# A two-layer transformer megakernel: layer 1's feed-forward one chunk later, and its convolution, residual addition and modulation in another order

## The reference, cut to what matters

```python
x = x + attn(cond(x, c))            # cond: modulated norm (scale, shift from c), 16-head attention of
                                    # width 16, o + o @ W_out; attn: layer norm, 16 rotary query heads
                                    # of width 128, one key/value head, causal softmax, @ Wo
y = causal_depthwise_conv(x, c)     # 32 taps per channel: 32 lags over 32 tokens
x = x + (relu(y @ w_fc) ** 2) @ w_proj     # 256 -> 1024 -> 256, weights block-quantised
```

## Time and profile before

| | us |
|---|---|
| median of 3 runs (lowest, highest) | 1431.28 (1430.86, 1431.62) |
| the profiled execution | 1429.93 |
| its span, first to last instruction | 1428.1 |
| busy in it: PE, DVE, ACT, POOL | 1306.4, 1125.2, 781.8, 137.8 |
| mean granted clock of PE | 0.974 |

### The profile page before, as it was taken

The page is one execution under the profiler, slowest core; times in us unless marked ns, Lnnn a source line. Parts: engine busy times, 40 slices in busy tenths (PEclk is TensorE's granted clock), DMA queues, the critical chain, the costliest instruction groups (busy, mean ns, idle before and its releaser), DMA issues.

```text
span 1428.1 us, 25862 instructions
## 1 busy us (share of the span) xinstructions
PE 1306.4 (91%) x9475; PEld 929.7 (65%) x9490; DVE 1125.2 (79%) x2892; ACT 781.8 (55%) x1486; POOL 137.8 (10%) x153
## 2 busy tenths in 40 slices
PE   5999999979799999999999858899999999999997
PEld 2444444658687877778777535566677767676766
DVE  4899999778968686786869798587869696969785
ACT  3999888854455565656555644534353434444213
POOL 0000000101010101011011110001010202020100
PEclk9999999989999999999999979898999999999999
DMA  9333333520111010202022300000000000000000
GB/s 380 105 71 74 71 89 87 148 95 31 38 38 46 31 46 31 73 4 75 21 104 85 129 24 1 28 11 8 9 19 3 22 0 22 7 8 8 8 8 15
DMA packets 26518, 73.97 MB, mean 52 GB/s; under 512 B 3992, under 2 KB 5156, under 8 KB 25136
## 3 DMA queue, kind: packets, MB, share of 16 engines
q1 hardware_dynamic: 25840, 71.62, 16.0%
q10 hardware_dynamic: 576, 0.98, 0.2%
HBM read 49.52 MB, written 23.07 MB: 51 GB/s over the span
## 4 chain that ended last, share of the span: by engine, by line
PE 51%; DVE 36%; ACT 6%; issue 6%; DMA 1%; DVEq 0%; SPq 0%; ACTq 0%; POOL 0%
PE psum L613 12%; PE psum L722 6%; DVE work L1811 5%; PE psum L934 5%; PE psum L661 4%; DVE ffn_mem L1928 4%; DVE h_all L1811 3%; DVE work L1942 3%; PE psum L963 3%; PE psum L973 3%; PE psum L880 2%; PE psum L626 2%; PE psum L671 2%; PE psum L647 1%; PE psum L567 1%
## 5 line engine op out<-in xcount | busy, mean ns | idle before, releaser
L613 PE MATMUL psum<-h_all,w_big 128*128 128x256 f32 x1024 | 244.1, 387 | 9.7 <-ACT work L1259 9.7
L613 PEld LDWEIGHTS psum<-h_all,w_big 128*128 128x128 f32 x1024 | 190.3, 192 | 49.4 <-issue 14.3
L1811 DVE SCALAR_TENSOR_TENSOR work<-work,taps 128x248 f32<-128x248 f32 (+30 forms) x558 | 149.3, 346 | 0.0
L567 PE MATMUL psum<-w_big,h_all 128*64 128x512 f32 x512 | 124.8, 609 | 0.0
L934 PE MATMUL psum<-work,w_big 128*128 128x256 f32 x512 | 117.3, 382 | 0.0
L1811 DVE SCALAR_TENSOR_TENSOR h_all<-h_all,taps 128x248 f32<-128x248 f32 (+30 forms) x434 | 116.6, 343 | 0.1
L722 PE MATMUL psum<-w_big,gru_mem 128*128 128x256 f32 x512 | 113.6, 379 | 0.5 <-ACT gru_mem L1301 0.5
L722 PEld LDWEIGHTS psum<-w_big,gru_mem 128*128 128x128 f32 x512 | 96.9, 190 | 14.7 <-ACT gru_mem L1301 0.6
L934 PEld LDWEIGHTS psum<-work,w_big 128*128 128x128 f32 x512 | 96.1, 191 | 15.2 <-DVE gru_mem L2348 2.5
L963 PE MATMUL psum<-w_big 128*128 128x256 f32 x448 | 105.4, 388 | 0.0
L963 PEld LDWEIGHTS psum<-w_big 128*128 128x128 f32 x448 | 84.4, 193 | 19.2 <-issue 8.4
(11 more groups left out here) (321 smaller groups left out, 2492.5 us busy)
## 6 DMA issues: line engine op xcount, KB each, us to landing
value_rows<-w_emb SPq DMA_DIRECT2D x128, 128.0 KB, 2.3
work<-value_rows SPq DMA_DIRECT2D x16, 1024.0 KB, 5.8
w_big<-in_Wq SPq DMA_DIRECT2D x2, 2048.0 KB, 17.1
w_big<-in_Wo SPq DMA_DIRECT2D x2, 2048.0 KB, 21.3
out<-w_big SPq DMA_DIRECT2D x15, 256.0 KB, 2.0
x_res<-out SPq DMA_DIRECT2D x15, 256.0 KB, 2.7
w_big<-in_Wv SPq DMA_DIRECT2D x1, 2048.0 KB, 19.0
w_big<-in_Wk SPq DMA_DIRECT2D x1, 2048.0 KB, 23.9
```

The lines of the kernel that those rows point to most:

```text
L567: mm = pe.matmul(bank(4 + n)[j * B:(j + 1) * B, :], h_all[:, k, :, 2 * pair + j], w_big[:, 2, k * H * HD + n * 512:k * H * HD + (n + 1) * ...
L613: mm = pe.matmul(bank(n % 2)[:, o * TA:(o + 1) * TA], w_big[:, s, k * H * HD + at:k * H * HD + at + HD], h_all[:, k, bass.ds(i * BA, BA), ...
L1811: ins = dve.scalar_tensor_tensor(dst[:, :, lag:], src[:, :, :T - lag], tap, dst[:, :, lag:], ALU.mult, ALU.add)
```

## The change

- The feed-forward's `fc` of chunks 0 to 5 leaves the end of step i and goes into step i+1, two tiles behind each pair of heads 2 to 9, into banks 6 and 7. Chunks 6 and 7 keep theirs at the end of steps 7 and 8. The relus (ACT) and squares (POOL) move with it. The output of the convolution gets a second buffer, used in turn.
- DVE: lags 0 to 2 go from the start of the step to behind cond's norms (in step 7 behind head 0); lag 3 goes from among the heads to behind them. Behind lags 10 to 19 come the layer norm, the addition of group 0, lags 20 to 22, the modulation, the addition of group 1, and lags 23 to 31.
- PE: group 1's projection is cut into 3, 3, 6 and 4 heads, where it was 5, 5 and 6.
- ACT: `keep_x3` comes after the copy of the values and waits for the convolution before; the row squares come before the second spreading; `keep_residual` comes before the norms' last parts.
- Step 7: the second half of `pj` of chunk 5 goes behind the turning of x3; the first 8 lags of chunk 7's convolution go ahead of the addition that ends chunk 5.
- The hardware loops of PE, ACT, POOL and DVE are written out.

```diff
-        y3_t = states[:, 512:1024].rearrange("p (k n) -> p k n", k=KD)
+        y3_homes = [area.rearrange("p (k n) -> p k n", k=KD) for area in (states[:, 512:1024], w_big[:, 2, 2048:2560])]
...
+        def fc_out(c, f):
+            return bank(f % 2)[:, 0:TA] if c >= NA - 2 else bank(6 + f % 2)[:, 0:TA]
...
-            def fc(c):
-                for f in range(KF):
+            def fc(c, tiles=range(KF)):
+                if 0 in tiles:
+                    pe.wait_ge(conv2_on.sem, 2 * T * c + 2 * T)
+                    if c < NA - 2:
+                        pe.wait_ge(xt2_on.sem, c + 2)
+                for f in tiles:
...
-                    if late:
-                        pe.wait_ge(relu_on.sem, KF * ni)
...
                 elif rot:
-                    q_heads(i, range(2, 10))
+                    for h in range(2, 10, 2):
+                        q_heads(i, range(h, h + 2))
+                        if late:
+                            fc(ni - 1, range(h - 2, h))
...
-                    if late:
+                    if late and cond:
                         pj(ni - 1, (1,))
...
                     if rot:
-                        rot_project(i, 1, range(0, 5))
+                        rot_project(i, 1, range(0, 5 if begun else 3))
                     cond_outputs(ci, 1)
                     if rot:
-                        rot_project(i, 1, range(5, 10))
+                        rot_project(i, 1, range(5, 10) if begun else range(3, 6))
                     cond_project(ci, 1)
+                    if rot and not begun:
+                        rot_project(i, 1, range(6, 12))
...
                 if rot and not cond:
                     turn_x3(i)
-                if ffn:
-                    pe.wait_ge(conv2_on.sem, 2 * T * ni + 2 * T)
+                    pj(ni - 1, (1,))
+                if ffn and ni >= NA - 2:
                     fc(ni)
...
-                    rot_project(i, 1, range(10, H))
+                    rot_project(i, 1, range(10 if begun else 12, H))
...
-            with pe.Fori(0, NA - 4) as last:
-                chunk1(last + 2, True, True, True, True, True)
+            for i in range(2, NA - 2):
+                chunk1(i, True, True, True, True, True)
...
             def keep_x3(c):
                 act.wait_ge(x3_turned.sem, c + 1)
+                if c and not (isinstance(c, int) and c == NA - 1):
+                    act.wait_ge(conv2_on.sem, 2 * T * c)
...
+                if late:
+                    relus(ni - 1, range(KF))
...
+                    if prep and not begun:
+                        row_squares(i + 2)
                     spread_cond_probs(ci, 1)
                     keep_cond_outputs(ci, 1)
+                if ffn and cond:
+                    keep_residual(ni)
...
-                if ffn:
-                    relu_squares(i - 1, range(0, 2))
+                if late:
+                    relu_squares(i - 2, range(KF))
...
                 def conv2(lags):
                     if ffn and rot:
+                        if 0 in lags and ni == 1:
+                            dve.wait_ge(y_out, 16)
+                        if 0 in lags and ni >= 2:
+                            dve.wait_ge(fc_sum.sem, KF * (ni - 1))
...
-                conv2(range(0, 3))
...
                     cond_norm(ci, 0, clink)
+                    conv2(range(0, 1))
                     turn_heads(1)
                     cond_norm(ci, 1, clink)
+                    if not begun:
+                        turn_heads(1)
+                    conv2(range(1, 3))
+                else:
+                    conv2(range(0, 3))
...
-                conv2(range(3, 4))
...
-                conv2(range(4, 7))
+                conv2(range(3, 7))
...
                 if rot and not cond:
                     conv2(range(7, T))
+                    add_attention1(i)
+                    conv(i, range(0, 8), *ffn1(i)[1:], xt2_on, 1, conv2_on, None)
...
-                    conv2(range(10, T))
+                    conv2(range(10, 20))
                 if cond:
                     layer_norm(ci, clink)
                     c_step.end_trip()
+                if rot and cond:
+                    if ffn:
+                        dve.wait_ge(res_on.sem, ni + 1)
+                    add_attention1(i, (0,))
+                if cond:
+                    conv2(range(20, 23))
                 if prep:
                     film_rows(i + 2, lambda ins: link(ins, c_step, i + 2))
+                if rot and cond:
+                    add_attention1(i, (1,))
+                if cond:
+                    conv2(range(23, T))
                 if rot and not cond:
-                    add_attention1(i)
-                    conv(i, range(T), *ffn1(i)[1:], xt2_on, 1, conv2_on, None)
+                    conv(i, range(8, T), *ffn1(i)[1:], xt2_on, 1, conv2_on, None)
```

More of the change, by code:

```diff
@@ L358, in ffn1 @@
                 return x_c, *(work[:, j * 512:(j + 1) * 512].rearrange("p (k n) -> p k n", k=KD) for j in range(2))
-            return x3_buf, x3_t, y3_t
+            return x3_buf, x3_t, y3_homes[c % 2]
+        def fc_out(c, f):
+            return bank(f % 2)[:, 0:TA] if c >= NA - 2 else bank(6 + f % 2)[:, 0:TA]
         def wo_out(c, g):
@@ L1556, in relus @@
                         act.wait_ge(h2_on.sem, KF * c + f - 1)
-                    act.activation(relu[:, f % 2, :], bank(f % 2)[:, 0:TA], ACT.Relu).then_inc(relu_on.sem, 1)
+                    act.activation(relu[:, f % 2, :], fc_out(c, f), ACT.Relu).then_inc(relu_on.sem, 1)
                     if own_squares(c):
@@ L1573, in chunk1 @@
                     keep_cond_qk(ci, 0, 1)
-                if ffn and rot:
-                    keep_x3(ni)
                 if begun:
@@ L1582, in chunk1 @@
                     act.activation(v1[:].rearrange("p g n -> p (g n)"), bank(0)[:, 0:GA * HD], ACT.Copy).then_inc(v1_on.sem, 1)
+                if ffn and rot:
+                    keep_x3(ni)
                 if cond:
                     keep_cond_v(ci)
+                if late:
+                    relus(ni - 1, range(KF))
                 if begun:
@@ L1615, in chunk1 @@
                     keep_cond_outputs(ci, 0)
+                    if prep and not begun:
+                        row_squares(i + 2)
                     spread_cond_probs(ci, 1)
                     keep_cond_outputs(ci, 1)
+                if ffn and cond:
+                    keep_residual(ni)
                 if rot and not cond:
                     keep_x3(i)
-                if ffn:
-                    relus(ni, range(0, 2))
-                if prep:
+                if ffn and ni >= NA - 2:
+                    relus(ni, range(KF))
+                if begun:
                     row_squares(i + 2)
-                if begun:
                     keep_w5(range(0, 4))
-                if ffn:
-                    relus(ni, range(2, 4))
                 if prep:
@@ L1631, in chunk1 @@
                     keep_w5(range(4, PIECES))
-                if ffn:
-                    relus(ni, range(4, KF))
                 if cond:
                     apply_norm(ci)
-                if ffn and cond:
-                    keep_residual(ni)
             keep_qk(0, range(0, 2))
@@ L1658, in _ @@
             chunk1(1, True, True, True, True, False)
-            with act.Fori(0, NA - 4) as last:
-                chunk1(last + 2, True, True, True, True, True)
+            for i in range(2, NA - 2):
+                chunk1(i, True, True, True, True, True)
             chunk1(NA - 2, True, True, True, False, True)
@@ L1781, in _ @@
             chunk1(1, True, True, True, True, False)
-            with pool.Fori(0, NA - 4) as last:
-                chunk1(last + 2, True, True, True, True, True)
+            for i in range(2, NA - 2):
+                chunk1(i, True, True, True, True, True)
             chunk1(NA - 2, True, True, True, False, True)
@@ L2366, in rot_soft_out, with add_attention1 @@
                 dve.transpose(p1_t[:, g, :], att1.rearrange("p e j -> p (e j)")).then_inc(p1_on.sem, 1)
-            def add_attention1(c):
-                dve.wait_ge(xr_in, 16 * c + 16)
-                for g in range(GA):
+            def add_attention1(c, groups=range(GA)):
+                if 0 in groups:
+                    dve.wait_ge(xr_in, 16 * c + 16)
+                for g in groups:
                     dve.wait_ge(wo1_sum.sem, GA * c + g + 1)
@@ L2475, in chunk1 @@
                                               ALU.add).then_inc(y_on.sem, 1)
-                if rot and cond:
-                    if ffn:
-                        dve.wait_ge(res_on.sem, ni + 1)
-                    add_attention1(i)
                 if rot:
@@ L2496, in _ @@
             chunk1(1, True, True, True, True, False)
-            with dve.Fori(0, NA - 4) as last:
-                chunk1(last + 2, True, True, True, True, True)
+            for i in range(2, NA - 2):
+                chunk1(i, True, True, True, True, True)
```

7 lines of the change are left out of this document (1 added, 6 removed).

## The result

The changed kernel takes 1415.04 us (median of 4 runs, 1414.20 to 1416.06) against 1431.45 us (4 runs, 1430.86 to 1432.17) of the kernel before on the same chip: ratio 0.9885, 95% interval [0.9873, 0.9898], 16.4 us faster. The forecast was 1418.6 us. The profiled execution took 1415.49 us with a span of 1413.7.

A forecast was written before the change was run, and what follows sets the result against it. PE was taken to bound each step of layer 1, so only its waits could be won. 15.5 - 3.2 + 6.8 - 6.4 = 12.7 us won; 1431.28 - 12.7 = 1418.6 us, range 1414.6 to 1424.0 us.

The forecast's parts named there:

- the five waits: At the end of steps 2 to 6 PE's waits of `fc` for the convolution, 11.4 us in all, would go.
- Steps 2 to 6: Layer 1's steps 2 to 6: 15.5 us would go and 3.2 us come, 0.65 a step.
- (b): Steps 2 to 6: the second cond outputs come two heads earlier, so PE waits 0.1 us for ACT's spreading.
- (a): Steps 2 to 6: lag 3 behind the last head makes PE's wait for the rotary softmax 0.55 us longer.
- (c): Steps 2 to 6: the layer norm is through before PE turns the next `xl`: no wait, 1.0 us to spare.
- (d): Steps 2 to 6: the modulation ends before its reader comes: no wait, 0.3 us to spare.
- the second rival: The cover of (c) or (d) is too short by 1 us in each of six steps: 1424.6 us; chance 0.12.
- Step 1: Step 1 loses 7.8 us of `fc`, its softmax wait grows by 1.0 us: net gain 6.8 us.
- Steps 7 and 8: The last two steps: `fc` of chunk 5 adds 7.07 us, less 0.7: 6.4 us lost.
- the first rival: Step 7: a lower PE clock behind its waits, costing 1.15 to 4.8 us: 1419.8 to 1423.4 us; chance 0.14.
- third: Rival: `fc` among the heads waits for late lags or its relu as long as before: 1430 us; chance 0.04.
- fourth: Rival: POOL's squares slow DVE's heads and lags, up to 3.5 us a step: 1439.7 us; chance 0.03.

The follow-up runs named there:

- Experiment 2: The kernel before with only its hardware loops on PE, ACT, POOL and DVE written out: 1429.22 us, ratio 0.9990.
- Experiment 4: The changed kernel with lag 3 done among the heads again, as before the change: 1411.71 us, ratio 0.9862.
- Experiment 1: The changed kernel with lags 10 to 31 in one stretch ahead of the layer norm again, `fc` staying among the heads: 1437.45 us, ratio 1.0045.
- experiment 8: Its gap-closing run: the third version of experiment 7 with two more `pj` products between step 7's output groups, two fewer behind the turning of x3: 1412.21 us.
- experiment 7: The change run again (1414.66 us) beside three versions of it on one chip: 1413.32, 1412.59 and 1407.95 us.
- experiment 3: The changed kernel with the squares of all layer 1 relus on ACT, none on POOL: 1413.52 us, ratio 0.9889.
- experiment 5: The changed kernel with the second half of chunk 5's `pj` back between step 7's rotary outputs: 1417.49 us, ratio 0.9909.
- experiment 6: The changed kernel with 16 idle products, read by nothing, in PE's softmax waits of step 1: 1414.17 us, ratio 0.9891.
- the third version of experiment 7: The changed kernel with step 7's second half of `pj` split around the outputs, and lag 3 back among the heads: 1412.59 us, ratio 0.9872.
- the fourth version: The third version of experiment 7 plus 16 idle products in step 1: 1407.95 us, ratio 0.9840.
- the second version of experiment 7: The changed kernel with four products of step 7's second half of `pj` ahead of the first outputs, four behind the turning of x3: 1413.32 us, ratio 0.9882.

## Why the prediction was right, and where it was off

**What bounds the kernel, and the five waits: right.** Steps are bound by PE, and its waits for the convolution went whole. Step 5's lost clock came back as its gap went, as foreseen: 69.87 us to 65.80. Experiment 2 takes some certainty from the reason: in it step 5 kept the clock with the gap there.

**Steps 2 to 6: 3.1 us more won than foreseen**, 0.62 a step (2.94 against 2.32 in step 3), from small terms of one sign, by the distances of starts in step 3. (1) From the first outputs (L960) to the step's end it is 9.94 us less, against 4 x 1.725 = 6.90 added among the heads: 3.04 won. I had 2.87: 2.25 and 0.72 less the 0.1 of (b), which didn't come. I took `fc`'s row of 7.07 us for its pace, but that row holds the tail of its last matmul. (2) From cond's first turning (L899, L896 before) to the first outputs it is 0.39 us more, for the 0.55 of (a). Experiment 4 puts (a) itself at 0.53, so it was right, and some 0.14 us was won beside it, for a reason not tried. (3) PE reached that turning 0.29 us sooner than the 6.90 us explain; before, it stood there behind DVE's norm, which had lags 0 to 2 ahead of it. I had not listed this gain, and that the lags were the cause was not tried.

**The cover (c), (d): right.** The norm found its lags done, with DVE waiting 0.64 us for PE; I had them end 0.5 us before its input came. Experiment 1 shows what the second rival would have been.

**Step 1: right**, -7.2 for -6.8 us, with two errors that cancel in part: the first outputs came 1.28 us later in the step, for 1.0, and from them to the end it was 8.5 us less, for 7.8.

**Steps 7 and 8: the step that failed**, +8.3 for +6.4 us. Its structure was right: the outputs came 7.4 us later, for 7.7 foreseen, and the last `fc` was held by PE and not by the convolution. Two terms were too small. From the start of the outputs to the projection I took 3.45 us (1372.1 to 1375.55), the time of ACT's first four copies; it was 4.39 (1355.19 to 1359.58), since the second outputs write to the banks that these empty, one by one. And the first rival came beside the forecast: 1.69 us in the projection, within its bounds of 1.15 and 4.8. The rest, 0.7 us, went the other way: 0.2 ahead of the outputs and 0.5 between the projection and the last `pj`. I gave the rival 0.14, arguing from waits of 2.25 and 2.57 us that had cost nothing. The whole trace of before has six waits of 2.2 to 2.6 us ahead of an `fc`, and one of them, of 2.24 us, cost anything; in experiment 2, the same program with its loops written out, three of six did. One in six is near 0.14, and four in twelve is over twice that: the count over one profile was weak ground. That the gains of the other steps made up for this loss was luck. The rule of the Trainium skill that I cited (TensorE: Matmul & The Clock Gate, "Why this matters for your kernels"), no idle gaps between bursts, agrees in direction: with the gap closed in experiment 8 the projection took 14.08 us. Experiments 2 and 7, where equal gaps ended differently, show that the length of the gap alone doesn't tell it.

**The other rivals: no.** The waits did not move (third); `fc` among the heads found its input and its relus done. The contention of POOL and DVE (fourth) is there, 0.9 us a step by experiment 3, and lies beneath the heads where DVE waits for PE. I had bounded it by 3.5. The Trainium skill (GPSIMD Engine Reference, "Key points") has POOL contend with DVE instructions that have two SBUF inputs; experiment 3 agrees, as the lags got faster and the rotations, with one input in PSUM, did not. The 0.5 us of a head's wait in step 1 is not of the squares, since POOL squares no relus there; DVE is busy without a break from before lag 0 until that head is turned, with 2.2 us of lags 0 to 2 in it, so the lags among the heads are the likely cause. No run took them out.

**The sum.** Of the 3.6 us by which I was too high, 3.1 are steps 2 to 6 and 0.4 step 1, less 1.9 in steps 7 and 8. Of the other 2.0, 1.8 come from setting a difference of two profiled executions against medians: the one of before was 1.35 us under the median that I used, that of after 0.45 over its own. The rest is the unchanged stretches (0.1) and rounding.

## What to carry to other kernels

Before work is moved out of a wait, ask what ran under it: `fc` at the end of the step was the cover of the next layer norm, and moving it pays only because 24 vector instructions were moved behind that norm too. Cost a row that goes between others by the distance of starts, not by its own length, and outputs that go into banks still being emptied by the copies' pace. Look at every gap ahead of a long row of matmuls, and count what closing it does at the next gap: experiments 5, 6 and 8 won at one place and lost half of it or more at another. And don't read from one profile which gap costs the clock: writing out the loops moved it from one step to three others.

## What the runs showed of the hardware

The granted clock fell behind waits of PE, but in these rows of steps 2 to 8 neither the length of a wait nor the work just ahead of it decides. Full clock was kept behind 2.25 and 2.57 us, 2.24 (step 5 of experiment 2), 1.43 (the last `fc` of the third version of experiment 7) and 0.82 us (the fourth version). It was lost behind 2.24 us, 2.25 and 2.23 (steps 2 and 3 of experiment 2), 1.67 and then 1.18 (the change), 1.19 alone (the second version of experiment 7), 3.17 (experiment 5), 2.30 (experiment 8) and 0.82 us (the third version). The change, profiled twice, lost it at the same rows, with 473.07 us from step 1 to the last `pj` both times. How far that holds for other executions is not known: the mean granted clock of the change's eight runs lies between 0.972 and 0.976, and that of the kernel before between 0.970 and 0.976. What besides the wait decides stays open.

Outputs that go into PSUM banks which ACT is still copying out run at the pace of the copies: four took 2.13 us at full clock beside copies of 0.5 us each (second outputs of step 7 in the change), and 1.14 us where the banks were free (the first outputs).
